# Block 0 of a graph attention's scores: masks by an identity matmul, the score bank copied by ScalarE, and a reordered opening

## Chip, cores and metric

One core of a Trainium2 chip runs the kernel. The metric is the time on the device in microseconds (us), as the median of several runs. Engines: TensorE (PE in the profile; PEld are its weight loads), VectorE (DVE), ScalarE (ACT), GpSimd (POOL) and SyncE (SP), whose queue issues all the DMAs.

## What is computed

One layer of graph attention over 4096 nodes of 256 features, followed by a feed-forward layer with eight experts. Cut to what matters here:

```python
h = layernorm(x)
lQ, lK, lV = masked_x @ Wlq, h @ Wlk, h @ Wlv + blv
s = where(adj, lQ @ lK.T / 16, -1e9)        # 4096 x 4096
g, e = (masked_x @ Wgq) @ (mean(h) @ Wgk).T / 16, masked_x @ Wes
m = maximum(max(s, 1), maximum(g, e))
le, ge, ee = exp(s - m), exp(g - m), exp(e - m)
den = sum(le, 1) + ge + ee
res = le/den @ lV + ge/den * gV + ee/den * eV
x1 = x + maximum(res, masked_x)
out = x1 + ffn(layernorm(x1))               # 8 experts, 256 -> 1024 -> 256
```

## The kernel before

The 4096 queries are cut into eight blocks of 512 (`CH`); for each block the 4096 keys pass in 32 tiles of 128 (`KT`). Step `t` makes one score tile, 128 keys by 512 queries, in one of three PSUM banks `s_ps[t % 3]` (`score`, L1528). Every fp32 product is split into a high part, rounded to the type fp32r, and a low remainder: `split_product` (L47) issues three matmuls for each half of the 256 features (L52, L53, L54), six for a score. The mask of a tile, `bias`, is 0 where the adjacency has an edge and a large negative number elsewhere; GpSimd makes it from bytes (`bias_of`, L696). VectorE adds it to the bank and writes the sum into a slot of `scores` (`mask`, L868), then folds it into the running maximum `kept_ps` (`keep`, L884). From step 37 on, the exponentials of the tiles (ScalarE, L1285 and L1291) and their products with the values (`weigh`, L1552 and L1559) run beside the scores of later blocks. The last block is followed by the experts.

Block 0 is different, and it is the first stage of the kernel: while its 32 scores are made, the keys themselves are still being made, in eight groups `g` of 512 nodes (`NG`), with four score tiles to a group. For group `g` the work goes through all engines:

- SP loads the rows, `load_x(g)` (L571), into one of two buffers `xg`.
- VectorE takes their moments (`first_moments`, L1129 and L1132), GpSimd the reciprocal deviation (`reciprocal_deviation`, L762 and L764, `rstd`), VectorE the product with the mean (`shift`, L1137, `nmr`).
- ScalarE normalises in four activations (`normalise`, L1443, line L1450, `lnf`), and writes the high part of the values (`high_values`, L1457, `vst`); GpSimd writes their low part in two halves (`low_values`, L776). SP stores `vst` to DRAM.
- TensorE transposes the rows through the identity, eight times 128x128 (`turn_keys`, L1762, into `u_ps`); ScalarE copies the two banks as high keys (L1469, `lnT_hi`), VectorE subtracts for the low keys (`low_turned`, L1153).

Each engine has its own program, an order written out by hand, and engines meet at semaphores only. The loops over `g` are at L619 (SP), L797 (GpSimd), L1176 (VectorE), L1466 (ScalarE) and L1781 (TensorE). In round `g` of its loop an engine works on the scores `t = 4g-4` to `4g-1` of the keys of group `g-1`, and on the keys of group `g` or of later groups. GpSimd's round is the mask of `t+2`, low values, the mask of `t+3`, low values, the mask of `t+4`, the reciprocal deviation of group `g+2`, the mask of `t+5`:

```python
low_values(g, 0); bias_of(t + 3); low_values(g, 1)
bias_of(t + 4); reciprocal_deviation(g + 2); bias_of(t + 5)
```

ScalarE's round is the high keys of `g`, `normalise(g + 1)`, which needs the reciprocal of group `g+1`, and `high_values(g)`.

Ahead of the loops stands an opening. The two query weights are multiplied to one matrix (`fold`, L1752), VectorE subtracts a column (`qw`, L1171), ScalarE and VectorE split it (`qw_hi`, `qw_lo`, L1465 and L1175). The masked tokens of block 0, `mg_raw`, are split too (`mg_hi` by ScalarE, L1300; `mg_lo` half by VectorE, L1144, half by GpSimd, L770), and `queries(0, m)` makes the queries of block 0 from them in twelve matmuls, into `mb_ps` and `mt_ps`; ScalarE and VectorE split those (L1304 and L1148). Then TensorE folds the key weights (`gw_ps`), makes a small attention column (`attc_ps`, L1795), transposes group 1, and begins the scores. The masked tokens of block 1 are loaded into the same `mg_raw` in round 1 (`load_masked`, L247) and split there; their queries follow in round 3. In round 1 VectorE also centres the value weights (L1215, L1217).

At the stage's end, after score 29, TensorE makes the mean's matmuls (L1812) and after score 31 the row products (L1820); VectorE takes the folded row `wg_b` (L1225) and goes on to the first maximum and the first exponentials.

## Time and profile before

| | |
|---|---|
| median of 3 runs | 1091.46 us (1090.68 to 1092.83) |
| the profiled execution | 1091.44 us, span 1089.6 us, granted clock 0.991 of full |
| TensorE | 1043.4 us busy, 96% of the span |
| VectorE | 864.3 us, 79% |
| GpSimd | 704.2 us, 65% |
| ScalarE | 542.7 us, 50% |
| bytes moved | 180.39 MB, 166 GB/s on average |
| first stage | from 0 to about 108 us; the first exponential of block 0 begins at 107.74 us |

All times in the trace count from the start of the span. A row of a timeline gives the start, the time, the engine, the line, the operation, the tensors written and read, and how many instructions were merged in it; where the engine stood idle before, how long and for whom stands in brackets. Start to start of two neighbours is what an instruction costs an engine that is never idle; the time of a single row is longer where instructions overlap.

### The profile page before, as it was taken

How to read it: one execution, taken by the hardware profiler on the slowest of the kernel's cores; microseconds unless marked ns; L12 is line 12 of the kernel's file. 1: busy time of each engine (PE TensorE's matmuls, PEld its weight loads, DVE VectorE, ACT ScalarE, POOL GpSimd, SP SyncE). 2: the span in 40 equal slices, each digit the busy share in tenths (PEclk: the TensorE clock that was granted, in tenths of full speed). 3: DMA queues.
4: the chain of work that ended last, by engine and by line, in shares of the span. 5: the costliest groups of instructions: out<-in, count | busy, mean ns of one | idle time of the engine just before them, and what ended most of it. 6: DMA issues, size and time to landing. Idle time of an engine off the chain costs nothing.

```text
span 1089.6 us, 15802 instructions
## 1 busy us (share of the span) xinstructions
PE 1043.4 (96%) x4996; PEld 869.2 (80%) x4996; DVE 864.3 (79%) x1534; ACT 542.7 (50%) x973; POOL 704.2 (65%) x713
## 2 busy tenths in 40 slices
PE   6878999999999999999999999998899999999998
PEld 5656887887887888788788788886787888898886
DVE  4999977798799789789879978987976775677653
ACT  4640444444445345444544444547467556655664
POOL 3774776767678677777767867768475455554451
PEclk9999999999999999999999999999899999999999
DMA  6585343453354345335335425449846547654621
GB/s 221 179 294 181 107 150 108 155 176 118 107 177 152 118 168 167 109 126 189 126 112 174 165 97 169 146 130 335 293 167 213 203 150 248 215 182 150 209 78 59
DMA packets 104341, 180.39 MB, mean 166 GB/s; under 512 B 14265, under 2 KB 45882, under 8 KB 104002
## 3 DMA queue, kind: packets, MB, share of 16 engines
q1 hardware_dynamic: 104258, 179.38, 48.8%
q8 instruction: 40, 0.66, 0.3%
q14 instruction: 43, 0.35, 0.1%
HBM read 143.63 MB, written 27.33 MB: 157 GB/s over the span
## 4 chain that ended last, share of the span: by engine, by line
PE 83%; DVE 5%; POOL 5%; DMA 3%; issue 2%; ACT 1%; SPq 0%; DVEq 0%; POOLq 0%; ACTq 0%
PE u_ps L1552 19%; PE s_ps L52 11%; PE s_ps L54 11%; PE s_ps L53 11%; PE u_ps L1559 9%; PE u_ps L52 3%; PE u_ps L54 3%; PE u_ps L53 3%; PE mt_ps L52 2%; PE mt_ps L54 2%; PE mt_ps L53 2%; POOL p_lo L709 2%; POOL m_lo L770 1%; PE s_ps L1607 1%; PE mb_ps L52 1%
## 5 line engine op out<-in xcount | busy, mean ns | idle before, releaser
L709 POOL TENSOR_TENSOR p_lo<-p_all,p_hi 128x512 fp32r<-128x512 f32 x224 | 295.4, 1319 | 171.8 <-PE u_ps L1559 105.2
L1285 ACT ACTIVATE p_hi<-scores 128x512 fp32r<-128x512 f32 x224 | 141.6, 632 | 360.3 <-DVE scores L866 360.0
L882 DVE TENSOR_TENSOR scores<-s_ps,bias 128x512 f32<-128x512 f32 x256 | 175.7, 686 | 84.0 <-PE s_ps L54 82.5
L1552 PE MATMUL u_ps<-p_hi,v_in 128*128 128x512 f32 x896 | 241.0, 391 | 0.0
L52 PE MATMUL s_ps<-q_hi,lnT_hi 128*128 128x512 f32 x512 | 203.0, 397 | 12.9 <-DVE scores L882 12.8
L54 PE MATMUL s_ps<-q_hi,lnT_lo 128*128 128x512 f32 x512 | 200.6, 392 | 0.0
L53 PE MATMUL s_ps<-q_lo,lnT_hi 128*128 128x512 f32 x512 | 200.4, 391 | 0.0
L1552 PEld LDWEIGHTS u_ps<-p_hi,v_in 128*128 128x128 f32 x896 | 167.2, 188 | 34.0
L701 POOL TENSOR_SCALAR bias<-adj 128x512 f32<-128x512 uint8 x256 | 164.2, 642 | 19.3 <-DVE scores L882 19.2
L866 DVE TENSOR_TENSOR scores<-scores,mb_ps 128x512 f32<-128x512 f32 x256 | 171.7, 677 | 0.8 <-PE mb_ps L1577 0.8
L903 DVE TENSOR_TENSOR kept_ps<-kept_ps,scores 128x512 f32<-128x512 f32 x232 | 162.3, 699 | 8.0
L1559 PE MATMUL u_ps<-p_lo,v_in 128*128 128x512 f32 x448 | 138.1, 389 | 0.2 <-POOL p_lo L709 0.2
L1291 ACT ACTIVATE p_all<-scores 128x512 f32<-128x512 f32 x224 | 138.0, 616 | 0.0
L731 POOL TENSOR_TENSOR e_lo<-raw,e_hi 128x512 fp32r<-128x512 f32 x64 | 84.2, 1319 | 73.5 <-ACT e_hi L1324 73.5
L52 PEld LDWEIGHTS s_ps<-q_hi,lnT_hi 128*128 128x128 f32 x512 | 96.7, 189 | 37.7 <-DVE scores L882 18.0
L54 PEld LDWEIGHTS s_ps<-q_hi,lnT_lo 128*128 128x128 f32 x512 | 96.8, 189 | 20.6
L53 PEld LDWEIGHTS s_ps<-q_lo,lnT_hi 128*128 128x128 f32 x512 | 96.9, 189 | 19.5
L1559 PEld LDWEIGHTS u_ps<-p_lo,v_in 128*128 128x128 f32 x448 | 84.0, 188 | 18.2 <-POOL p_lo L709 0.6
L52 PE MATMUL u_ps<-h_hi,e_hi 128*128 128x512 f32 x128 | 50.5, 394 | 0.1
L53 PE MATMUL u_ps<-h_lo,e_hi 128*128 128x512 f32 x128 | 50.4, 393 | 0.0
L54 PE MATMUL u_ps<-h_hi,e_lo 128*128 128x512 f32 x128 | 50.3, 393 | 0.0
L965 DVE TENSOR_TENSOR h_lo<-mb_ps,h_hi 128x512 fp32r<-128x512 f32 x32 | 22.1, 690 | 29.6 <-ACT h_hi L1324 29.6
(212 smaller groups left out, 1777.0 us busy)
## 6 DMA issues: line engine op xcount, KB each, us to landing
v_in<-v_scratch SPq DMA_DIRECT2D x118, 512.0 KB, 3.7
adj<-in_adj SPq DMA_DIRECT2D x64, 256.0 KB, 3.9
raw<-in_wffn SPq DMA_DIRECT2D x32, 512.0 KB, 4.9
v_scratch<-vst SPq DMA_DIRECT2D x8, 1024.0 KB, 6.2
mx<-in_mx SPq DMA_DIRECT2D x18, 256.0 KB, 6.8
xg<-in_x SPq DMA_DIRECT2D x8, 512.0 KB, 4.4
uhi_scratch<-uT_high SPq DMA_DIRECT2D x8, 512.0 KB, 2.7
ulo_scratch<-uT_low SPq DMA_DIRECT2D x8, 512.0 KB, 3.6
```

The source lines that it names most:

```text
L52: nc.tensor.matmul(out, l_hi, r_hi, start=start and k == 0, stop=False)
L53: nc.tensor.matmul(out, l_hi, r_lo, start=False, stop=False)
L54: last = nc.tensor.matmul(out, l_lo, r_hi, start=False, stop=stop and k == n - 1)
L701: nc.gpsimd.tensor_scalar(bias[:, t % 2], adj8[:, t // 4 % 2, t % 4 * CH:(t % 4 + 1) * CH], -MASKED, MASKED, ALU.mult, ALU.add).then_inc(b ...
L709: nc.gpsimd.tensor_tensor(out=low_part(y), in0=whole_part(y), in1=high_part(y).bitcast(fp32), op=ALU.subtract).then_inc(plo_ready, 1)
L866: nc.vector.tensor_tensor(scores[:, y % SLOTS], scores[:, y % SLOTS], mb_ps[:, :], ALU.subtract).then_inc(centred, 1)
L882: nc.vector.tensor_tensor(scores[:, t % SLOTS], s_ps[t % 3][:, :], bias[:, t % 2], ALU.add).then_inc(masked, 1)
L903: nc.vector.tensor_tensor(top_keys[:, :] if k == LASTS else kept_ps[:, :], kept_ps[:, :], scores[:, t % SLOTS], ALU.max).then_inc(kept, 1)
L1285: nc.scalar.activation(high_part(y), scores[:, y % SLOTS], ACT.Exp, scale=SCALE).then_inc(phi_ready, 1)
L1291: nc.scalar.activation(whole_part(y), scores[:, y % SLOTS], ACT.Exp, scale=SCALE).then_inc(pall_ready, 1)
L1552: nc.tensor.matmul(u_ps[d][:, :], values[:, x % 2, at:at + P], high_part(x), start=k == 0 and part == 0, stop=False)
L1559: last = nc.tensor.matmul(u_ps[d][:, :], values[:, x % 2, d * P:(d + 1) * P], low_part(x), start=False, stop=k == LASTS)
```

## The change

The masks of block 0 are written as fp32r into `turned_bias`, which lies where `bias` lies. `score` adds the mask by a seventh matmul into the same bank, with an fp32r copy of the identity, `ident_high`, as the weights. VectorE's `mask` falls away for block 0, and ScalarE copies the bank into its slot instead (`keep_score`). The masked value becomes a power of two. `bias_of` waits for the score two tiles back in place of its mask. `normalise` is cut into two halves with a copy between them.

The opening is put in another order. ScalarE begins with the masked tokens of block 0 and the identity's copy; the query weights' split goes by halves and stands ahead of `first_moments(1)` on VectorE; both halves of `mg_lo` of block 0 go to GpSimd, which also makes the masks of tiles 0 and 1 and the reciprocal deviation of group 2 ahead of its loop. The key weights' fold, the attention column and the transposes of group 1 go behind scores 0 and 1 on TensorE, in other banks. SP loads group 2's rows ahead of four weight matrices, after the first normalising. Centring the value weights goes from VectorE to GpSimd (`centred_values`). `first_moments(2)`, `shift` and `low_turned` change their places on VectorE, and the last of the first three value loads waits for score 31, as `ident_high` lies where it lands.

```diff
...
 SCALE = 1.0 / 16.0
-MASKED = -1.0e9 / SCALE
+MASKED = -float(2 ** 34)
 EPS = 1e-5
...
 bias = rings("bias", [P, 2, CH])
+turned_bias = nc.alloc_sbuf_tensor_at("turned_bias", [P, 2, CH], fp32r, offset=q_at + 8 * SLOT + 4 * CH * 2)
 mxt = rings("mxt", [P, D])
...
 vst = before("vst", [P, 2, TG, 2 * D], fp32r)
+ident_high = before("ident_high", [P, P], fp32r)
...
 tr_ps, q_ps = u_ps, [mb_ps, mt_ps]
-qw_ps, gw_ps, attc_ps = s_ps
+qw_ps, gw_ps, attc_ps = s_ps[0], mb_ps, mt_ps
...
 phi_ready, pall_ready, plo_ready, pv_done = (sem(n) for n in ("phi_ready", "pall_ready", "plo_ready", "pv_done"))
-late_low_ready = sem("late_low_ready")
+late_low_ready, ident_high_ready = sem("late_low_ready"), sem("ident_high_ready")
 turned, local_ready, top_ready, spread_ready, spread_done = (
...
         sp.dma_start(wq_in[:, n], kblocks(w)).then_inc(wg_loaded, 16)
+    sp.wait_ge(ln_ready, 1)
+    load_x(2)
     for n, w in enumerate((wlv, wev, attn_wT, next_wT)):
...
     sp.dma_start(blv_row[:, :], blv[None, :]).then_inc(wlv_loaded, 16)
-if g + 2 < NG:
+if 0 < g < NG - 2:
     sp.wait_ge(ln_ready, g + 1)
...
 for i in range(VRING):
+    if i == VRING - 1:
+        sp.wait_ge(score_done, KT)
     load_values(sp, i)
...
     pool.wait_ge(adj_in[g % 2], 16 * (g // 2) + 16)
-wait(pool, masked, t - 1)
-nc.gpsimd.tensor_scalar(bias[:, t % 2], adj8[:, t // 4 % 2, t % 4 * CH:(t % 4 + 1) * CH], -MASKED, MASKED,
+wait(pool, score_done if t < KT else masked, t - 1)
+nc.gpsimd.tensor_scalar(turned_bias[:, t % 2] if t < KT else bias[:, t % 2], adj8[:, t // 4 % 2, t % 4 * CH:(t % 4 + 1) * CH], -MASKED, MASKED,
                         ALU.mult, ALU.add).then_inc(bias_ready, 1)
...
+def centred_values():
+    pool.wait_ge(w_loaded, 64)
+    pool.wait_ge(wlv_loaded, 32)
+    for k in range(KD):
+        nc.gpsimd.tensor_tensor(out=w_all[:, WLV, k], in0=w_all[:, WLV, k], in1=wlv0_b[:, :],
+                                op=ALU.subtract).then_inc(wlv_ready, 1)
+    pool.wait_ge(wlv_ready, 2)
+    nc.gpsimd.tensor_copy(w_all[0:1, WLV, 0, :], blv_row[:, :]).then_inc(wlv_ready, 1)
 def low_weight_matrix(n):
...
 reciprocal_deviation(0)
-low_queries_input(0, 0)
+for k in range(KD):
+    low_queries_input(0, k)
+bias_of(0)
+bias_of(1)
 reciprocal_deviation(1)
+reciprocal_deviation(2)
 for g in range(NG + 1):
...
     low_values(g, 1)
-bias_of(t + 4)
-if g + 2 < NG:
+if g > 0:
+    bias_of(t + 4)
+if 0 < g and g + 2 < NG:
     reciprocal_deviation(g + 2)
-if g < NG:
+if 0 < g < NG:
     bias_of(t + 5)
...
     low_queries_input(1, 0)
+    centred_values()
 if g == 3:
...
 dve.wait_ge(bias_ready, t + 1)
-if t == 16:
-    dve.wait_ge(wlo_ready, 4)
-if t == 20:
-    dve.wait_ge(w_stored, 32)
 if t == 32:
...
 shift(0)
-first_moments(1)
 dve.wait_ge(qw_done, 1)
...
                             ALU.subtract).then_inc(qw_ready, 1)
-low_queries_input(0)
-dve.wait_ge(qwhi_ready, 1)
-nc.vector.tensor_tensor(qw_lo[:, :, :], qw[:, :, :], qw_hi[:, :, :].bitcast(fp32), ALU.subtract).then_inc(qwlo_ready, 1)
+for m in range(KD):
+    dve.wait_ge(qwhi_ready, m + 1)
+    nc.vector.tensor_tensor(qw_lo[:, m], qw[:, m], qw_hi[:, m].bitcast(fp32), ALU.subtract).then_inc(qwlo_ready, 1)
+first_moments(1)
 for g in range(NG + 1):
     t = 4 * g - 4
-    if g + 1 < NG:
-        shift(g + 1)
     if g == NG:
...
 for i in range(4):
+    if i == 0 and 0 < g and g + 1 < NG:
+        shift(g + 1)
+    if i == 0 and 1 < g < NG:
+        low_turned(g, 0)
+        low_turned(g, 1)
     if g > 0:
-        mask(t + i)
         keep(t + i)
-    if i == 0 and g < NG:
+    if i == (1 if g == 1 else 0) and g < 2:
         for k in range(KD):
             low_turned(g, k)
+        if g == 0:
+            shift(1)
     if i == 1 and 0 < g and g + 2 < NG:
...
         low_queries(0, k)
+    first_moments(2)
+if g == 1:
     dve.wait_ge(attc_done, 1)
...
     nc.vector.tensor_tensor(attc_c[:, :], attc_ps[:, 0:KD], attnb_c[:, :], ALU.add).then_inc(attcol_ready, 1)
-    first_moments(2)
-if g == 1:
-    dve.wait_ge(w_loaded, 64)
-    dve.wait_ge(wlv_loaded, 32)
-    for k in range(KD):
-        nc.vector.tensor_tensor(w_all[:, WLV, k], w_all[:, WLV, k], wlv0_b[:, :], ALU.subtract).then_inc(wlv_ready, 1)
-    dve.wait_ge(wlv_ready, 2)
-    nc.vector.tensor_copy(w_all[0:1, WLV, 0, :], blv_row[:, :]).then_inc(wlv_ready, 1)
 if g in (6, 7):
...
-def normalise(g):
+def keep_score(t):
+    act.wait_ge(score_done, t + 1)
+    if t == 16:
+        act.wait_ge(wlo_ready, 4)
+    if t == 20:
+        act.wait_ge(w_stored, 32)
+    nc.scalar.activation(scores[:, t], s_ps[t % 3][:, :], ACT.Copy).then_inc(masked, 1)
+def normalise(g, tiles=range(TG)):
...
     wait(act, vlo_ready, 2 * g - 2)
-    for j in range(TG):
+    for j in tiles:
         last = nc.scalar.activation(lnf[g % 2][:, j, 1:D], xg[:, g % 2, j, 1:D], ACT.Identity, scale=rstd[:, g % 2, j:j + 1],
                                     bias=nmr[:, g % 2, j:j + 1])
-    last.then_inc(ln_ready, 1)
+    if TG - 1 in tiles:
+        last.then_inc(ln_ready, 1)
...
+high_queries_input(0)
+act.wait_ge(ident_ready, 2)
+nc.scalar.activation(ident_high[:, :], ident[:, :], ACT.Copy).then_inc(ident_high_ready, 1)
 normalise(0)
-high_queries_input(0)
-act.wait_ge(qw_ready, 2)
-nc.scalar.activation(qw_hi[:, :, :], qw[:, :, :], ACT.Copy).then_inc(qwhi_ready, 1)
+for m in range(KD):
+    act.wait_ge(qw_ready, m + 1)
+    nc.scalar.activation(qw_hi[:, m], qw[:, m], ACT.Copy).then_inc(qwhi_ready, 1)
 for g in range(NG):
+    t = 4 * g - 4
+    if g > 1:
+        keep_score(t - 1)
+    if g == 1:
+        keep_score(0)
+        keep_score(1)
     for k in range(KD):
...
                              accum_out=xsum[:, k, g:g + 1]).then_inc(thi_ready, 1)
-    if g + 1 < NG:
-        normalise(g + 1)
     if g == 0:
...
             high_queries(0, k)
+    if g + 1 < NG:
+        normalise(g + 1, range(2))
+    if g > 1:
+        keep_score(t)
+    if g + 1 < NG:
+        normalise(g + 1, range(2, TG))
+    if g > 1:
+        keep_score(t + 1)
+    if g == 1:
         act.wait_ge(gw_done, 1)
...
             high_queries(1, k)
+    if g > 0:
+        keep_score(t + 2)
+for t in range(KT - 5, KT):
+    keep_score(t)
 for t in range(KT, STEPS):
...
 wait(pe, masked, t - 2)
+if t < KT and t % 4 == 0:
+    pe.wait_ge(tlo_ready, t // 2 + 2)
 ks = slice(k * P, (k + 1) * P)
-split_product(nc, s_ps[t % 3][:, :], [(lnT_hi[:, d, ks], lnT_lo[:, d, ks]) for d in range(KD)],
-              [(q_hi[:, n % 2, d], q_lo[:, n % 2, d]) for d in range(KD)]).then_inc(score_done, 1)
+last = split_product(nc, s_ps[t % 3][:, :], [(lnT_hi[:, d, ks], lnT_lo[:, d, ks]) for d in range(KD)],
+                     [(q_hi[:, n % 2, d], q_lo[:, n % 2, d]) for d in range(KD)], stop=t >= KT)
+if t < KT:
+    pe.wait_ge(bias_ready, t + 1)
+    pe.wait_ge(ident_high_ready, 1)
+    last = nc.tensor.matmul(s_ps[t % 3][:, :], ident_high[:, :], turned_bias[:, t % 2], start=False, stop=True)
+last.then_inc(score_done, 1)
...
 t = 4 * g - 4
-if g < NG:
+if g < NG and g != 1:
     turn_keys(g)
 if g == 0:
-    pe.wait_ge(qwlo_ready, 1)
+    pe.wait_ge(qwlo_ready, 2)
     queries(0, 0)
     queries(0, 1)
-    pe.wait_ge(wg_loaded, 32)
-    fold(gw_ps, gw_done)
-    pe.wait_ge(rows_loaded, 16 * 3)
-    pe.wait_ge(w_loaded, 64)
-    for m in range(KD):
-        for k in range(KD):
-            last = nc.tensor.matmul(attc_ps[:, m:m + 1], w_all[:, WATT, k, m * P:(m + 1) * P], lnb[:, k:k + 1],
-                                    start=k == 0, stop=k == KD - 1)
-    last.then_inc(attc_done, 1)
-if g == 1:
-    pe.wait_ge(gw_ready, 1)
-    pe.wait_ge(attcol_ready, 1)
 if g > 0:
...
     score(t + 1)
+    if g == 1:
+        turn_keys(1)
+        pe.wait_ge(wg_loaded, 32)
+        fold(gw_ps, gw_done)
+        pe.wait_ge(rows_loaded, 16 * 3)
+        pe.wait_ge(w_loaded, 64)
+        for m in range(KD):
+            for k in range(KD):
+                last = nc.tensor.matmul(attc_ps[:, m:m + 1], w_all[:, WATT, k, m * P:(m + 1) * P], lnb[:, k:k + 1],
+                                        start=k == 0, stop=k == KD - 1)
+        last.then_inc(attc_done, 1)
     if g == 3:
+        pe.wait_ge(gw_ready, 1)
+        pe.wait_ge(attcol_ready, 1)
         queries(1, 0)
```

## Rows read from the trace of the kernel before

**Rows 1.** The page's first part: busy time, share of the span, instructions.
```profile
PE 1043.4 (96%) x4996; PEld 869.2 (80%) x4996; DVE 864.3 (79%) x1534; ACT 542.7 (50%) x973; POOL 704.2 (65%) x713
```

**Rows 2.** Windows: stretch, length, busy time (instructions) of PE, PEld, DVE, ACT, POOL.
```profile
50.00:55.00 5.00, 5.00 (x28) 4.22 (x27) 4.90 (x14) 2.82 (x7) 4.22 (x6) 1.00 0.33 89
```

**Rows 3.** The page's costliest groups: the mask; busy us, mean ns, idle before.
```profile
L882 DVE TENSOR_TENSOR scores<-s_ps,bias 128x512 f32<-128x512 f32 x256 | 175.7, 686 | 84.0 <-PE s_ps L54 82.5
```

**Rows 4.** The chain that ended last, 45 to 56 us: start, time, what.
```profile
45.89 1.04 POOL rstd L764
46.95 0.59 DVE nmr L1137
...
48.07 1.57 ACT lnf_even L1450 x3
49.65 0.96 ACT vst L1457
50.67 1.29 POOL vst L776
51.97 0.58 POOL bias L701
52.55 1.18 POOL vst L776
53.84 0.62 POOL bias L701
54.74 1.04 POOL rstd L764
```

**Rows 5.** GpSimd's timeline: the reciprocal deviations of groups 3 and 7.
```profile
34.98 1.04 POOL L764 TENSOR_TENSOR rstd<-veps,mhalf 128x4 f32<-128x4 f32 x1
...
74.85 1.04 POOL L764 TENSOR_TENSOR rstd<-veps,mhalf 128x4 f32<-128x4 f32 x1
```

**Rows 6.** TensorE's timeline: two neighbouring score matmuls, and eight transposes.
```profile
49.10 0.39 PE L52 MATMUL s_ps<-q_hi,lnT_hi 128*128 128x512 f32 x1
49.33 0.39 PE L53 MATMUL s_ps<-q_lo,lnT_hi 128*128 128x512 f32 x1
...
51.83 1.03 PE L1762 MATMUL u_ps<-ident,lnf_even 128*128 128x128 f32 x8
```

**Rows 7.** ScalarE's timeline: two neighbouring copies of a whole bank; the isolated one.
```profile
18.63 0.60 ACT L1304 ACTIVATE q_hi<-mt_ps 128x512 fp32r<-128x512 f32 x1 [0.97 <-PE mt_ps L54]
...
50.50 0.58 ACT L1304 ACTIVATE q_hi<-mb_ps 128x512 fp32r<-128x512 f32 x1
50.98 0.58 ACT L1304 ACTIVATE q_hi<-mt_ps 128x512 fp32r<-128x512 f32 x1
```

**Rows 8.** Opening: transposes, queries' first and last matmul, first score, second masked tokens.
```profile
10.68 1.58 PE L1762 MATMUL u_ps<-ident,lnf_even 128*128 128x128 f32 x8 [0.50 <-ACT lnf_even L1450]
...
14.04 0.50 PE L52 MATMUL mb_ps<-mg_hi,qw_hi 128*128 128x512 f32 x1 [1.78 <-DVE qw_lo L1175]
...
17.97 0.63 PE L54 MATMUL mt_ps<-mg_hi,qw_lo 128*128 128x512 f32 x1
...
21.85 0.48 PE L52 MATMUL s_ps<-q_hi,lnT_hi 128*128 128x512 f32 x1
...
31.19 1.06 ACT L1300 ACTIVATE mg_hi<-mg_raw 128x1024 fp32r<-128x1024 f32 x1 [1.05 <-DMA mg_raw<-in_mxT]
```

**Rows 9.** Timelines of VectorE and ScalarE: the folded row, the first exponential.
```profile
99.47 0.42 DVE L1225 COPY wg_b<-mt_ps 128x256 f32<-128x256 f32 x1 [0.38 <-PE mt_ps L1820]
...
107.74 0.63 ACT L1285 ACTIVATE p_hi<-scores 128x512 fp32r<-128x512 f32 x1 [24.05 <-DVE scores L866]
```

**Rows 10.** TensorE after two idle gaps; below, a window (length, busy, granted clock).
```profile
39.34 0.80 PE L52 MATMUL s_ps<-q_hi,lnT_hi 128*128 128x512 f32 x1 [2.23 <-DVE scores L882]
...
63.79 0.50 PE L52 MATMUL s_ps<-q_hi,lnT_hi 128*128 128x512 f32 x1 [2.27 <-DVE scores L882]
...
16.00:17.00 1.00, 1.00 (x4) 0.50 0.93 324
```

## The prediction, made before the change was run

> **What bounds the kernel now.** I read the page first. TensorE is busy 1043.4 us, 96% of the span [rows 1], and the change touches only the stage at the start, the scores of block 0 (tiles 0 to 31), so the question is when that stage ends. Next come the windows: from 50 to 55 us VectorE is busy 4.90 of 5 us [rows 2], so it looks like the bound of the stage; one mask costs it 0.686 us [rows 3]. The chain of waits then shows a second bound of the same size [rows 4]. It is a ring through three engines that closes once per group of four tiles: GpSimd's reciprocal deviation (`rstd`), VectorE's shift (`nmr`), ScalarE's four normalising activations (`lnf`) and its high copy (`vst`), GpSimd's low values, mask, low values, mask, and the next reciprocal. Each row begins where the one above ends. The reciprocal ends at 46.93 and one turn later at 55.78: 8.85 us. In other groups VectorE comes late and stretches the turn: the reciprocals of groups 3 and 7 end at 36.02 and 75.89 [rows 5], 39.87 us for four turns, 9.97 each. So relieving VectorE pays only down to the ring's own length, and whatever enters the ring is paid in every turn.
>
> **What the change moves.** The 32 masks leave VectorE, 32 x 0.686 = 22 us; of its 8.85 us per turn about 6.1 are left, and it binds no more. In their place come an identity matmul and `keep_score`, a copy on ScalarE. The matmul is bounded by the spacing of matmuls of its shape, 0.23 us, and by twice that at half clock; I take 0.23, as the clock is full in most windows. A score is then 7 x 0.23 = 1.6 us, a turn of TensorE 4 x 1.6 + 1.0 for eight transposes = 7.4 us [rows 6], under the ring. The copy's bounds are 0.60 us, a whole row of such a bank, and zero, as nothing excludes that one hides in a wait; I take 0.48, the spacing of two neighbours [rows 7], since it stands between other activations. Two of the four copies sit in the ring, one between the halves of the normalising and one ahead of the high copy, as ScalarE goes through its work in order. The other two fall where it waits for the next reciprocal.
>
> **The new ring.** Reciprocal's end to ScalarE 0.65, normalising 2.0, two copies 0.96, high copy with hand-over 1.1, low values 1.3, mask 0.58, low values 1.3, mask 0.58, reciprocal 1.35 [rows 4, 7]: 9.8 us. Are the scores in time? With the reciprocal's end at 0, the group's first score ends at -0.4 and its copy can start at 1.65; the second ends at 1.2 and is wanted at 3.15. The third and fourth wait longer: GpSimd writes the fourth mask only after low values, at 6.6, and TensorE, done with that score's six products at 4.2, stands 2.4 us at the identity matmul, with the next group's transposes and scores queued behind it. That idle time hides the identity matmuls (0.9 us per turn); without it TensorE would need 7.4 us, still less than the ring. ScalarE's next item is the copy of that fourth score; behind it are queued the turned keys' high copies, done at 8.7, where normalising can't start before 10.4: 1.7 us to spare. A turn of 9.8 against 9.97: the steady part is nearly even.
>
> **The opening.** The masked tokens' copy comes first (1.06), then the identity's (0.25, between 0.48 and nothing), then normalising, so the first transposes move from 10.68 to 11.7. The query weights no longer wait behind group 1's moments, and both low halves of the tokens go to GpSimd, so the query products follow the transposes at once, at 13.2 in place of 14.04 [rows 8]. Twelve take 2.8 us at full clock, to 16.0; before, they ended at 18.6, the later ones in 0.63 us each. A copy 0.6, a low half 0.7, and what VectorE has queued ahead (moments of group 1, low turned keys, shift) end at 17.5; the first score starts at 17.7 in place of 21.85, as the fold of the key weights, the attention column and the second transposes now stand behind two scores. Those end at 20.9, transposes 21.9, two turned banks' copies 23.1 (0.6 each), normalising 25.1, the folded weights' copy 25.7, the high copy 26.65, and with the 5.3 us of GpSimd's part of the ring the reciprocal of group 3 ends at 32.0 in place of 36.0: 4.0 ahead.
>
> In the next turn ScalarE first meets the second block's masked tokens, whose copy began at 31.19 when their load landed [rows 8]. The load is issued some 1.4 us earlier, so 29.8 now; then that copy 1.06, two score copies, the turned keys and the ring, to 42.2, 4.7 ahead of 46.93. Three turns of 9.8 against 28.96 us (46.93 to 75.89) give back 0.45: group 7's reciprocal ends at 71.7, 4.2 ahead.
>
> **The rest of the stage.** From 75.89 to the folded row on VectorE at 99.47 are 23.6 us [rows 5, 9]. Now: the ring's part up to the fourth mask, and score 23's end, 6.85; transposes 1.0; two scores 3.2; copy, high copy, low values, mask and score 27's end 3.9; low values, mask, score 28's end 1.95; score 29 1.6; the mean's matmuls 0.8; two scores 3.2; row products and hand-over 1.9: 24.4. That gives back 0.8. From the folded row to the first exponential at 107.74 [rows 9] nothing changes. So the stage ends 3.4 us earlier.
>
> **The clock.** TensorE stood idle 2.23 us ahead of 39.34, and the next matmul took 0.80 us; it stood idle 2.27 us ahead of 63.79, and the next took 0.50. From 16 to 17 us the granted clock was 0.50, the lower level of 1.2 GHz [rows 10], after a gap of 1.78 us [rows 8]. So gaps of about 2 us end either way. A stretch at the lower level costs some 1.6 us of matmuls. The new opening has a gap of 1.7 us ahead of the first score: if the clock falls there, scores and transposes end 1.7 later, of which 1.3 lasts, the next turn being held by the load. Bounds 0 and 1.3; the rows fell both ways, so 0.6. In later turns such a stretch is hidden by the 1.9 us that the second score has to spare.
>
> The Trainium skill, "TensorE: Matmul & The Clock Gate", section "HAM oscillation — how this bites in real kernels", says that matmul bursts with a wait behind each can be put back to the lower clock in every round. By that rule the sum would be the slower rival's 1098 us, by the rows 1088.6; the trace agrees in one of the two gaps above 2 us.
>
> **Edits costed at nothing.** Group 2's rows and a wait of SP for the first normalising go ahead of the weights' loads, which land about 1 us later; the copy that wants them first comes at 19.6, a cover of some 0.5 us. `centred_values` on GpSimd instead of VectorE: two subtractions of 0.64 (half of low values' columns and time) to 1.3 us, hidden while ScalarE is at its copies ahead of group 2's high copy; without that cover up to 2.9 us enter one turn. The early masks run while GpSimd waits for group 1's moments. The last value load now waits for score 31, long before its first product. Masks as a matmul operand: 0.62 us as now, or at most 1.3 as low values write that type; I take 0.62, as the operation stays the same; at 1.3 two masks would add 1.4 per turn. The constant costs nothing.
>
> The profiled execution took 1091.44 us, 1.84 more than its span of 1089.6; the median is 1091.46, so no correction is due. 1091.44 - 3.4 + 0.6 = 1088.6 us.
>
> **Rivals.** *Nothing to be measured, 0.25.* ScalarE now carries score copies and keys behind the masked tokens' copy; if that load lands at 31.2 as before, the turn ends 1.4 later, and with the lower clock at the first score 0.7 of the gain is left: 1090.7. For it: the queue carries the same bytes in less time. Against it: the transfers ahead are issued earlier.
>
> *Slower, 0.13.* TensorE's clock falls in every turn. Its wait of 2.4 us for the fourth mask recurs in five turns. If the whole burst behind it (14 matmuls, eight transposes) ran at 1.2 GHz, it would be 3.8 us longer, and the group's second score would end at 5.0 instead of 1.2; past 3.15 it holds ScalarE, so 1.9 per turn, 9.5 in all: 1098. It decides once a burst loses over 1.9 us; the 1.6 of one stretch doesn't. This is the case of the skill's rule above.
>
> **How the numbers follow.** The forecast has 0.62. About 0.2%, 2.2 us, is what a measurement of this kernel can tell from no change. Some 0.07 of the forecast falls within that, where the clock's full 1.3 is paid (1089.3): faster 0.55, same 0.32, slower 0.13. Range: at the low end the sum without the clock, 1088.0, less 1.5, a third of what ten copies in the ring cost (4.8), in case some hide; at the high end just past no change, for masks a little longer than 0.62: 1086.5 to 1092.0. It leaves out the slower rival and little else.
>
> **What would show it.** Right: first score near 17.7; reciprocals ending near 32, 42, 52, 62 and 72; ScalarE without a wait inside the ring; TensorE waiting for a mask once per group; VectorE idle about a third of a turn; first exponential near 104.9. Wrong: turns under 9.3 us (copies hide) or over 10.5 (clock, or longer masks), or ScalarE held by the masked tokens past 31.

## The result, and the profile after

The change made the kernel slower. It took 1098.48 us (median of 6 runs, 1095.52 to 1101.11) where the kernel before took 1091.22 (6 runs), a ratio of 1.0071 with a 95% interval of 1.0055 to 1.0088. A second set gave 1.0054 (1.0033 to 1.0074). The forecast was 1088.6, in a range of 1086.5 to 1092.0. The execution whose profile follows took 1100.55 us, 2.1 above its median, with a span of 1098.5.

TensorE's busy time, of the changed kernel, for [rows 1]:

```profile
PE 1049.5 (96%) x5028; PEld 875.2 (80%) x5028; DVE 836.2 (76%) x1499; ACT 559.6 (51%) x1007; POOL 708.8 (65%) x717
```

The window from 50 to 55 us, for [rows 2] (length, then busy time and instructions of PE, PEld, DVE, ACT, POOL; granted clock, DMA share, GB/s):

```profile
50.00:55.00 5.00, 5.00 (x24) 4.08 (x23) 3.54 (x11) 3.70 (x7) 2.62 (x3) 1.00 0.17 66
```

VectorE is relieved as intended: 3.54 of 5 us in place of 4.90. GpSimd's timeline of the changed kernel shows the ring, for [rows 4, 5] (start, time, engine, line, operation, and in brackets the idle time ahead and what ended it):

```profile
35.17 1.03 POOL L770 TENSOR_TENSOR rstd<-veps,mhalf 128x4 f32<-128x4 f32 x1
36.28 0.68 POOL L707 TENSOR_SCALAR turned_bias<-adj 128x512 fp32r<-128x512 uint8 x1
37.05 1.29 POOL L776 TENSOR_TENSOR mg_lo<-mg_raw,mg_hi 128x512 fp32r<-128x512 f32 x1
...
46.88 1.04 POOL L770 TENSOR_TENSOR rstd<-veps,mhalf 128x4 f32<-128x4 f32 x1
48.00 1.32 POOL L707 TENSOR_SCALAR turned_bias<-adj 128x512 fp32r<-128x512 uint8 x2
52.22 1.30 POOL L782 TENSOR_TENSOR vst<-lnf_odd,vst 128x512 fp32r<-128x512 f32 x1 [2.90 <-ACT vst L1482]
53.60 0.62 POOL L707 TENSOR_SCALAR turned_bias<-adj 128x512 fp32r<-128x512 uint8 x1
54.30 1.29 POOL L782 TENSOR_TENSOR vst<-lnf_odd,vst 128x512 fp32r<-128x512 f32 x1
55.67 0.62 POOL L707 TENSOR_SCALAR turned_bias<-adj 128x512 fp32r<-128x512 uint8 x1
56.37 0.23 POOL L768 TENSOR_SCALAR veps<-mv 128x4 f32<-128x4 f32 x1
56.69 1.03 POOL L770 TENSOR_TENSOR rstd<-veps,mhalf 128x4 f32<-128x4 f32 x1
```

The reciprocal ends at 47.92 and again at 57.72: a turn of 9.80 us, where 9.8 was forecast and [rows 4] had 8.85. But group 3's ended at 36.20, where 32.0 was forecast and the kernel before had 36.02, and from group 3 to group 4 it took 11.72 us, not 10.2. ScalarE's timeline tells why, and ends with the first exponential, for [rows 8, 9]:

```profile
33.62 1.06 ACT L1316 ACTIVATE mg_hi<-mg_raw 128x1024 fp32r<-128x1024 f32 x1 [2.98 <-DMA mg_raw<-in_mxT]
34.59 1.06 ACT L1465 ACTIVATE scores<-s_ps 128x512 f32<-128x512 f32 x2
...
48.15 1.09 ACT L1474 ACTIVATE lnf_even<-xg,nmr,rstd 128x255 f32<-128x255 f32 x2 [1.39 <-DVE nmr L1155]
49.15 0.58 ACT L1465 ACTIVATE scores<-s_ps 128x512 f32<-128x512 f32 x1
49.63 1.08 ACT L1474 ACTIVATE lnf_even<-xg,nmr,rstd 128x255 f32<-128x255 f32 x2
50.61 0.58 ACT L1465 ACTIVATE scores<-s_ps 128x512 f32<-128x512 f32 x1
51.09 1.05 ACT L1482 ACTIVATE vst<-lnf_odd 128x1024 fp32r<-128x1024 f32 x1
...
111.12 0.63 ACT L1301 ACTIVATE p_hi<-scores 128x512 fp32r<-128x512 f32 x1 [9.46 <-DVE scores L888]
```

The second block's masked tokens land at 33.62, and the score copies wait behind their copy. From 48.15 to 52.04 ScalarE runs without a gap: that is the ring, and two score copies stand in it, 0.48 us apart from their neighbours. VectorE's timeline shows who waited for those copies, and what the last turn waited for:

```profile
35.20 0.70 DVE L921 TENSOR_TENSOR kept_ps<-kept_ps,scores 128x512 f32<-128x512 f32 x1 [6.38 <-ACT scores L1465]
...
37.07 1.28 DVE L1155 SCALAR_TENSOR_TENSOR nmr<-mv,rstd 128x4 f32<-128x4 f32 x1
...
47.95 0.16 DVE L1155 SCALAR_TENSOR_TENSOR nmr<-mv,rstd 128x4 f32<-128x4 f32 x1 [1.61 <-POOL rstd L770]
...
75.34 1.40 DVE L1147 BATCH_NORM_STATS2 st<-xg 128x6 f32<-128x256 f32 x4 [3.84 <-DMA xg<-in_x]
...
102.86 0.42 DVE L1241 COPY wg_b<-mt_ps 128x256 f32<-128x256 f32 x1 [0.48 <-PE mt_ps L1873]
```

The running maximum (`kept_ps`) idled 6.38 us for ScalarE, and the shift (`nmr`), queued behind it, came at 37.07, 0.87 after its reciprocal. At 75.34 the moments of group 7 waited 3.84 us for their tokens; the turn that holds them took 11.08 us. SyncE's queue has the issues of both loads:

```profile
27.05 0.38 SPq L591 DMA_DIRECT2D v_scratch<-vst  x1
27.47 1.60 SPq L249 DMA_DIRECT2D mg_raw<-in_mxT  x2
...
64.42 0.43 SPq L601 DMA_DIRECT2D whi_scratch<-w_high  x1
64.89 0.43 SPq L602 DMA_DIRECT2D wlo_scratch<-w_low  x1
65.37 1.11 SPq L573 DMA_DIRECT2D xg<-in_x  x1
```

The masked tokens' load goes out at 27.47 behind a value store that waits for GpSimd's low values; the load of group 7's tokens goes out at 65.37 behind both stores of the weights. TensorE's timeline gives the opening:

```profile
15.04 0.63 PE L53 MATMUL mb_ps<-mg_lo,qw_hi 128*128 128x512 f32 x1
15.47 0.63 PE L54 MATMUL mb_ps<-mg_hi,qw_lo 128*128 128x512 f32 x1
...
20.91 0.50 PE L52 MATMUL s_ps<-q_hi,lnT_hi 128*128 128x512 f32 x1 [1.41 <-DVE q_lo L1166]
```

The first score starts at 20.91, not 17.7. ScalarE's first activation is one cause: it stood 7.51 us waiting for the masked tokens of block 0, whose copy is now ahead of everything else there.

```profile
9.51 1.06 ACT L1316 ACTIVATE mg_hi<-mg_raw 128x1024 fp32r<-128x1024 f32 x1 [7.51 <-DMA mg_raw<-in_mxT]
```

The first exponential comes at 111.12, 3.38 later than in [rows 9]; the span is 8.9 longer.

The rest of the difference lies behind the stage, which the change was not to touch. GpSimd's timeline near 640 us, first of the kernel before, then of the changed one:

```profile
639.26 1.29 POOL L709 TENSOR_TENSOR p_lo<-p_all,p_hi 128x512 fp32r<-128x512 f32 x1 [2.20 <-PE u_ps L1559]
640.52 0.62 POOL L701 TENSOR_SCALAR bias<-adj 128x512 f32<-128x512 uint8 x1
```

```profile
639.84 1.29 POOL L715 TENSOR_TENSOR p_lo<-p_all,p_hi 128x512 fp32r<-128x512 f32 x1 [0.72 <-PE u_ps L1611]
641.22 0.62 POOL L707 TENSOR_SCALAR bias<-adj 128x512 f32<-128x512 uint8 x1
```

From the low part of the weights to the mask it takes 1.26 us before and 1.38 after, though both durations are the same, 1.29 and 0.62. About 0.11 us of nothing stands ahead of each mask, and as much behind it. A block's period (from one block's normalised sum, `uT`, to the next) is 91.78 us before (200.34 to 292.12) and 91.97 after (203.88 to 295.85); over the five periods up to 660 us that is 1.1 us. Behind 740 us this one profile loses another 4 us, which no other run shows in this size (e13 below).

### The profile page after: what moved, and what is told of

It is laid out like the page before. It is cut to its first block, busy times and chain, and to the rows that moved or that the text cites. A ratio compares the mean times of both kernels' runs of the same rounds, so it can differ in the third digit from the quotient of the medians.

```text
span 1098.5 us, 15893 instructions
## 1 busy us (share of the span) xinstructions
PE 1049.5 (96%) x5028; PEld 875.2 (80%) x5028; DVE 836.2 (76%) x1499; ACT 559.6 (51%) x1007; POOL 708.8 (65%) x717
## 4 chain that ended last, share of the span: by engine, by line
PE 65%; DVE 12%; POOL 7%; issue 7%; ACT 4%; DMA 4%; SPq 0%; DVEq 0%; POOLq 0%; ACTq 0%
PE u_ps L1604 13%; PE s_ps L52 8%; PE s_ps L54 8%; PE s_ps L53 8%; PE u_ps L1611 7%; DVE scores L888 3%; POOL p_lo L715 2%; PE u_ps L52 2%; PE u_ps L53 2%; PE u_ps L54 2%; ACT p_all L1307 2%; PE mt_ps L52 2%; DVE kt_out L989 2%; PE mt_ps L54 2%; PE mt_ps L53 2%
## 5 line engine op out<-in xcount | busy, mean ns | idle before, releaser
L900 DVE TENSOR_TENSOR scores<-s_ps,bias 128x512 f32<-128x512 f32 x224 | 153.8, 687 | 89.0 <-PE s_ps L54 87.5
L707 POOL TENSOR_SCALAR bias<-adj 128x512 f32<-128x512 uint8 x224 | 141.4, 631 | 27.3 <-DVE scores L900 5.8
L715 POOL TENSOR_TENSOR low_scores<-scores,p_late 128x512 fp32r<-128x512 f32 x23 | 30.9, 1357 | 23.3 <-ACT scores L1307 23.2
```

The lines of the kernel that those rows point to most:

```text
L707: nc.gpsimd.tensor_scalar(turned_bias[:, t % 2] if t < KT else bias[:, t % 2], adj8[:, t // 4 % 2, t % 4 * CH:(t % 4 + 1) * CH], -MASKED, ...
L715: nc.gpsimd.tensor_tensor(out=low_part(y), in0=whole_part(y), in1=high_part(y).bitcast(fp32), op=ALU.subtract).then_inc(plo_ready, 1)
L900: nc.vector.tensor_tensor(scores[:, t % SLOTS], s_ps[t % 3][:, :], bias[:, t % 2], ALU.add).then_inc(masked, 1)
```

## The experiments

Eight of the kernels answer three questions in all eight combinations (the cube, below): do the two ring copies stand in the ring, is the constant -2^34 or the old -1.6e10, are two loads late (as in the change) or early. "Tokens" is the start of the first masked tokens' copy, where ScalarE waits for their load, and "First exp." the start of the first exponential, in the one profile of each; the ratio is to the kernel before on the same chip, with its 95% interval. The medians of different rows come from different chips, so rows are compared by their ratios.

| run | masks on | copies in ring | constant | loads | median us (runs) | ratio | tokens | first exp. |
|---|---|---|---|---|---|---|---|---|
| before | VectorE | - | old | late | 1091.22 (6) | 1 | - | 107.74 |
| changed | TensorE | yes | -2^34 | late | 1098.48 (6) | 1.0071 (1.0055 to 1.0088) | 9.51 | 111.12 |
| e13, the same | TensorE | yes | -2^34 | late | 1096.79 (6) | 1.0054 (1.0033 to 1.0074) | 9.55 | 112.29 |
| e2 | TensorE | yes | old | late | 1094.57 (8) | 1.0031 (1.0017 to 1.0044) | 9.34 | 108.83 |
| e10 | TensorE | yes | -2^34 | early | 1092.65 (12) | 1.0026 (1.0008 to 1.0043) | 8.95 | 108.89 |
| e14 | TensorE | yes | old | early | 1090.47 (12) | 0.9996 (0.9984 to 1.0008) | 7.66 | 105.75 |
| e3 | TensorE | no | -2^34 | late | 1090.62 (11) | 0.9996 (0.9986 to 1.0007) | 8.55 | 105.50 |
| e15 | TensorE | no | -2^34 | early | 1088.67 (12) | 0.9993 (0.9978 to 1.0008) | 7.91 | 102.40 |
| e5 | TensorE | no | old | late | 1089.83 (12) | 0.9988 (0.9975 to 1.0000) | 8.84 | 107.92 |
| e9 | TensorE | no | old | early | 1085.05 (6) | 0.9950 (0.9932 to 0.9968) | 7.61 | 101.86 |
| e4 | VectorE | - | old | late | 1088.39 (12) | 0.9974 (0.9962 to 0.9986) | 7.80 | 104.11 |
| e6 | VectorE | - | old | early | 1087.30 (12) | 0.9965 (0.9952 to 0.9978) | 8.71 | 103.43 |
| e1 (kernel before) | VectorE | - | -2^34 | late | 1092.87 (11) | 1.0010 (0.9996 to 1.0023) | - | 109.06 |

The load of the first masked tokens is issued at 2.27 or 2.28 us in every profile that has a time there, and yet its tokens land between 7.61 and 9.55. No edit touches it. So first exponentials of single profiles can differ by up to 1.9 us for that reason alone.

**e1: the constant alone**, in the kernel before.

```
-MASKED = -1.0e9 / SCALE
+MASKED = -float(2 ** 34)
```

> The kernel before with one edit: the masked value is -2^34 instead of -1.6e10. In the changed kernel's trace every mask that GpSimd makes has a gap of some 0.11 us ahead of it and behind it, in the main loop too, where only the constant differs, and a block takes 91.97 us instead of 91.78. Theory A, the constant makes GpSimd's mask slower: the gaps and the 91.97 us appear here, the ring's turns grow by 0.4 us, and the time rises by some 2 to 3 us, to 1093 to 1094.5. Theory B, the mask's new output type or GpSimd's new order does it: no gaps, 91.78 us per block, 1091.

Measured: 1092.87 us, 1.0010. The gaps are there: low part to mask 1.39 us (637.57 to 638.96), period 91.96 in the mean of five. So the value of the constant makes the gaps; the edit changes two numbers of the mask's instruction and nothing else. Theory A's growth of the ring did not come: the turn from group 4 to 5 is 8.86 us, as with the old constant (8.85, [rows 4]); the last section says why. In total time e1 is not told apart from no change.

**e2: the changed kernel with the old constant**, the same line the other way.

> The changed kernel with the old masked value, -1.6e10 (rounded by the matmul, still far below any score). Theory A (constant): the gaps vanish, a block takes 91.78 us again, the ring's turn falls from 9.8 to 9.4 us, the time falls by 1.3 (blocks) plus 1.5 to 2 (stage), to some 1095. Theory B (type or order): gaps and times as in the changed kernel, 1098.5.

Measured: 1094.57 us, 1.0031, no gaps, period 91.78. The constant accounts for a part; 0.31 of the 0.71% is left. The turn did not fall to 9.4 us as theory A had it: from group 3 on the turns are 11.42, 10.23, 9.98 and 9.80.

**e3: the two ring copies behind the high copy** (constant of the change).

```
-                    if g + 1 < NG:
-                        normalise(g + 1, range(2))
-                    if g > 1:
-                        keep_score(t)
...
+                    if g + 1 < NG:
+                        normalise(g + 1)
...
                     high_values(g)
+                    if g > 1:
+                        keep_score(t)
+                        keep_score(t + 1)
```

> The changed kernel with one edit on ScalarE: both score copies that stand inside the ring (one between the halves of the normalising, one ahead of the high copy) go behind the high copy. Ring theory: a turn falls by 0.96 us from 9.8 to some 8.85; over five turns up to 4.8 less, of which the turn that waits for the last rows' load gives back one or two: 1094.5 to 1096. Rival, TensorE or the clock sets the turns: turns of 9.8 as before, 1098.5.

Measured: 1090.62 us, 0.9996: the loss is gone, and more of it than the 1094.5 to 1096 us expected. The turn from group 4 to 5 is 8.85 us (44.64 to 53.49), the ring of [rows 4] again. The three others, 10.80, 9.60 and 11.52, are not; and of the 5.6 us between this profile's first exponential and the changed kernel's, 2.4 lie ahead of group 3's reciprocal (33.84 against 36.20), where the edit changes nothing.

**e4: the opening alone**: the change's order of the opening, with masks and score tiles on VectorE as before, no identity matmul, no copies, the old constant.

```
-                        last = nc.tensor.matmul(s_ps[t % 3][:, :], ident_high[:, :], turned_bias[:, t % 2], start=False, stop=True)
...
+                            mask(t + i)
                             keep(t + i)
...
-                        keep_score(t)
```

> The changed kernel's opening, its loads' order and its GpSimd order, with the masks on VectorE as in the kernel before (no identity matmul, no score copies, old constant). If the opening as such gains nothing, because the masked tokens' load and the half clock hold it: the reciprocal of group 3 ends near 36 us and the time is 1090 to 1092; then the whole loss of the changed kernel comes from the masks' move and the constant. If the opening itself costs: over 1094. If it gains what the prediction said: 1088.

Measured: 1088.39 us, 0.9974. The opening by itself gains 2.8 us; the masks' way to TensorE, as the change has it, then costs 0.57% (e2 less e4), 6.2 us.

**e5: e3 with the old constant.**

> The changed kernel with both of its faults taken out: the two score copies of a turn stand behind ScalarE's high copy, outside the ring, and the constant is -1.6e10 again; masks still go through the identity matmul and the scores still come from ScalarE. Theory A (the two faults are all that the change loses): the constant was worth 1.8 us on the kernel before and 3.9 on the changed one, so some 2 to 3.9 us come off the 1090.6 us of the run with the copies behind: 1087 to 1088.6, at or below the 1088.4 of the opening alone; GpSimd's mask to the next mask's start 0.59 instead of 0.70 us; turns of about 8.85 us from group 4 on and a period of 91.78 us per block. Theory B (masks on TensorE are worse than on VectorE even outside the ring, because TensorE waits in order for GpSimd's mask and the bursts run at the lower clock): 1090 us or more, turns of 9.5 us or more, above the opening alone by over 1 us.

Measured: 1089.83 us, 0.9988, between the two theories. Without both faults the version still stands 0.14% above the opening alone, which the two intervals do not tell apart. Its turns point to loads: the masked tokens' copy begins at 32.98, and the last turn takes 11.95 us.

**e6: the opening alone, with two moves in SyncE's queue**: the second masked tokens' load ahead of the value store, the weights' stores behind the load of group 7's tokens.

```
                         load_x(g + 2)
+                    if g == 1:
+                        sp.wait_ge(q_done, 2)
+                        load_masked(sp, 1)
+                    if g == 5:
+                        sp.wait_ge(wlo_ready, 4)
+                        sp.dma_start(whi_dram, ...)
+                        sp.dma_start(wlo_dram, ...)
                     if g > 0:
                         sp.wait_ge(vlo_ready, 2 * g)
```

> The opening alone (masks on VectorE, old constant), with two moves in SP's queue: the second masked tokens' load is issued ahead of the value store instead of behind it, so some 4 us earlier (19.7 instead of 24.1 us), and the two stores of the weights go behind the load of group 7's tokens instead of ahead. Theory A (the loads hold the turns 2 to 3 and 6 to 7): the masked tokens' copy starts near 27.3 instead of 30.4 us, group 4's reciprocal ends 1 to 2 us earlier than 42.96, group 7's moments start 1 to 2 us earlier than 67.47; 1085 to 1087.5 us against 1088.4. Theory B (both loads are hidden, as the reciprocal of group 3 ended at 32.40 and hangs on GpSimd and VectorE, not on the masked tokens): the copy starts earlier and nothing behind it moves by over 0.5 us: 1088 to 1089.

Measured: 1087.30 us, 0.9965. The last turn is 8.85 us (62.41 to 71.26) in place of 10.09, and the four turns up to group 7 take 37.05 us in place of 39.56, but the time is only 0.09% better than e4's, less than the two intervals tell apart.

**e7, e8, e11, e12: which constants make the gaps**, in the kernel before, one run each: `MASKED` = -2^33, -1.7e10, -2^35, -2.0e10.

> The kernel before with the constant -2^33 in place of -1.6e10. It is a power of two like the change's -2^34, but smaller than the old constant. Theory A (a power of two as the immediate slows GpSimd's mask): the gap of 0.11 us on both sides of each mask is there, mask to next mask's start 0.72 us in the main loop, period 91.97 us per block, some 1093 us. Theory B (it is the size, or the exponent of 34): no gaps, 0.59 to 0.62 us, period 91.78, some 1091 us.

> The kernel before with the constant -1.7e10 in place of -1.6e10: no power of two, and close to the change's -2^34 = -1.718e10. Theory A (a power of two as the immediate slows GpSimd's mask): no gaps, period 91.78 us per block, some 1091 us. Theory B (the size decides, somewhere between 1.6e10 and 1.718e10, or any other constant than the old one does it): gaps of 0.11 us on both sides of each mask, period 91.97, some 1093 us. If neither this nor -2^33 shows gaps, the exponent of 34 or the value itself is left.

> The kernel before with the constant -2^35. Of -1.6e10, -1.7e10 and -2^33 none had the gaps around GpSimd's masks, -2^34 had. Theory A (from 2^34 on in size they appear): gaps of 0.11 us on both sides of each mask, period 91.97 us per block, some 1093 us. Theory B (only -2^34 has them): none, period 91.78.

> The kernel before with the constant -2.0e10, over 2^34 in size and no power of two. Theory A (from 2^34 on in size the gaps appear): gaps of 0.11 us on both sides of each mask, period 91.97 us per block, some 1093 us. Theory B (only a power of two from 2^34 on, or only -2^34): none, period 91.78, some 1091 us.

GpSimd's timeline, of e8 (-1.7e10) and of e12 (-2.0e10):

```profile
641.74 1.29 POOL L709 TENSOR_TENSOR p_lo<-p_all,p_hi 128x512 fp32r<-128x512 f32 x1 [0.84 <-PE u_ps L1559]
643.00 0.62 POOL L701 TENSOR_SCALAR bias<-adj 128x512 f32<-128x512 uint8 x1
```

```profile
642.01 1.29 POOL L709 TENSOR_TENSOR p_lo<-p_all,p_hi 128x512 fp32r<-128x512 f32 x1 [0.72 <-PE u_ps L1559]
643.39 0.62 POOL L701 TENSOR_SCALAR bias<-adj 128x512 f32<-128x512 uint8 x1
```

-2^33 and -1.7e10 leave 1.26 us from start to start, like -1.6e10; -2.0e10 and -2^35 leave 1.38 and 1.39, like -2^34. Being a power of two is not what counts: the gaps appear from some size between 1.70e10 and 1.718e10 (2^34) on. The periods go with them: 91.80 and 91.78 us without, 91.96 and 91.99 with. Each run's single time (1092.22, 1089.51, 1089.34, 1092.85) says nothing; runs of one kernel differ by more.

**e9: e5 with the early loads**, and **e10: the changed kernel with the early loads**, both by e6's edit.

> The changed kernel with the copies behind the ring, the old constant, and the two moves in SP's queue (second masked tokens' load ahead of the value store, weight stores behind group 7's load). Theory A (in the run with the copies behind and the old constant the masked tokens' copy at 32.98 us still held ScalarE's score copies, and the load of group 7 made the turn 6 to 7 11.95 us): both go, the copy starts near 29, group 4's reciprocal ends near 43, the last turn takes under 10.2; 1085.5 to 1087.5 us, level with the 1087.3 of the opening with early loads. Theory B (masks on TensorE cost by themselves, as the run without the loads' moves stood 1.4 us above the opening alone): 1088 to 1089.5 us, above the opening with early loads by 1 us or more.

> The changed kernel as it is, with only the two moves in SP's queue. Theory A (what the prediction's first rival named, the masked tokens' load that stands ahead of the score copies on ScalarE, is a part of the loss, 1.5 us, and the load of group 7, turn 11.08 instead of 9.8, another 1.3): masked tokens' copy near 29.5 instead of 33.6 us, group 4's reciprocal 2 to 3 us earlier against the first score, last turn 9.8 to 10; 1094.5 to 1096.5 us. Theory B (the loads are not on the path, all of the loss is the copies in the ring and the constant): 1097.5 us or more.

Measured: e9 1085.05 us, 0.9950, theory A, and the fastest of all; e10 1092.65, 1.0026. ScalarE's timeline of e10 (its load went out at 21.03):

```profile
29.02 1.05 ACT L1316 ACTIVATE mg_hi<-mg_raw 128x1024 fp32r<-128x1024 f32 x1
29.97 0.58 ACT L1465 ACTIVATE scores<-s_ps 128x512 f32<-128x512 f32 x1
```

The masked tokens no longer hold it: no wait stands ahead of 29.02, and the turns up to group 7 are 10.20, 9.80, 9.81 and 9.76 us where the change had 11.72, 9.80, 9.79 and 11.08. Those turns are 2.8 us shorter, as theory A had it; by time the loads' order is worth 0.28 or 0.45%, by which of the change's two ratios one takes.

**e13: the changed kernel again; e14: only the copies in the ring; e15: only the constant.**

> The changed kernel, unchanged, a second time. Theory A (its loss is steady and made up of the parts found): 5 to 8 us above the kernel before, and in this profile the stretch from the first exponential to the end is 981 to 984 us, as in all other profiles with or without the constant, not the 987.4 of its first profile. Theory B (the change costs something late in the kernel too): again 986 us or more for that stretch.

> The changed kernel with the old constant and the two moves in SP's queue, so that of the three suspects only the score copies between ScalarE's ring steps are left (two of the four of a turn). Theory A (ten copies of 0.48 us are paid in full, as the prediction had it): 4.8 us above the version with the copies behind and the same loads (0.995 of the kernel before), so 0.999 to 1.000 of the kernel before; turns of 9.8 us. Theory B (with the loads early most of them hide): within 2 us of 0.995; turns of 9.3 us or less.

> The version with the copies behind the ring and the early loads, with the constant -2^34 put back, so that of the three suspects only the constant is left. Theory A (the gaps cost 0.19 us in each of seven block periods and the shift that slips in ahead of the mask gives back in the ring what the gaps take): 1 to 2 us above 0.995 of the kernel before, so 0.996 to 0.997; turns as long as without it, within 0.2 us. Theory B (the gaps cost 0.46 us in each of the five turns too): 3 us or more above, 0.998 or more.

Measured: e13 1096.79 us, 1.0054. From its first exponential to its end are 984.7 us, between the theories: 2.7 less than in the change's first profile, 2.8 more than in the kernel before. Most of those 4 us came and went, so I don't count them as the change's. Its turns are 11.72, 10.23, 9.99 and 10.96 us: in the second, a copy in the ring waited for its score (0.17 us ahead of 48.45), which the first profile doesn't show.

e14 gave 0.9996, 0.46% above e9, 5.0 us: by its time theory A. Two reciprocals of e14, of groups 5 and 6, on GpSimd's timeline:

```profile
52.21 1.03 POOL L770 TENSOR_TENSOR rstd<-veps,mhalf 128x4 f32<-128x4 f32 x1
61.94 1.04 POOL L770 TENSOR_TENSOR rstd<-veps,mhalf 128x4 f32<-128x4 f32 x1
```

That is a turn of 9.74 us, in all four the same within 0.06. But e9, with the copies out of the ring, does not turn in 8.85 us: its turns are 9.28, 9.25, 10.12 and 9.42. From group 3's reciprocal to group 7's e14 takes 38.92 us and e9 38.07, 0.85 less, where eight copies paid in full make 3.84; another 2.27 lie between group 7's reciprocal and the first exponential (33.08 and 30.81). In e10 and e15, the same pair with the new constant, it is 1.54 and 3.66. So the copies cost what was forecast for them, within the intervals, but not by 0.96 us in every turn: without them something else sets the turn. VectorE's timeline of e9 shows it for group 6:

```profile
51.67 0.70 DVE L921 TENSOR_TENSOR kept_ps<-kept_ps,scores 128x512 f32<-128x512 f32 x1 [0.89 <-ACT scores L1465]
52.28 1.11 DVE L1155 SCALAR_TENSOR_TENSOR nmr<-mv,rstd 128x4 f32<-128x4 f32 x1
```

The reciprocal had ended at 51.51. The shift is queued behind the running maximum, which waits for the last score's copy on ScalarE, and begins 0.77 us late.

e15 gave 0.9993, by its time theory B, by its turns theory A: 33.86 to 71.89 is 38.03 us for four turns, and e9 took 38.07 (32.98 to 71.05). So the gaps do not lengthen the ring.

**The cube.** Each question has four pairs of runs that differ in nothing else (for the changed kernel the mean of its two ratios, 1.0063). Copies in the ring: 0.67, 0.33, 0.43 and 0.46%, in the mean 0.47%, 5.2 us. The constant: 0.32, 0.30, 0.08 and 0.43%, 0.28%, 3.1 us. The late loads: 0.37, 0.35, 0.03 and 0.38%, 0.28%, 3.1 us. With intervals of some 0.13% on each ratio, such a mean is uncertain by about 0.1%, 1.1 us. Together with e9's -0.50% the sum is 0.53%, against 0.71 and 0.54% measured: the three parts add up to the loss. The changed kernel is itself in a quarter of the pairs; without those pairs the sum is 0.43%, which the intervals still allow.

One thing the cube does not separate. In all four pairs for the loads the first masked tokens landed later in the profile with the late loads (by 0.6 to 1.7 us, 1.0 in the mean), and in all four pairs for the copies later with the copies in the ring (0.05 to 1.04, 0.6 in the mean), though neither edit comes before that landing; e4 and e6 differ the other way (7.80 and 8.71). With one or two profiles of a kernel it can't be told whether this is chance. If it isn't, up to 1.0 of the loads' 3.1 us and 0.6 of the copies' 5.2 belong to the landing.

## Why the prediction was wrong

**The ring's sum stood, and the price of what enters it in part by luck.** A turn of 9.8 was forecast; the two that no load stretched took 9.80 and 9.79 in the first profile, 10.23 and 9.99 in e13's, and 9.7 in e14. Ten copies at 0.48 us were priced at 4.8 us, and the runs gave 5.2 and, for e14 against e9, 5.0. But "whatever enters the ring is paid in every turn" did not hold: taken out again, the copies gave back 0.85 and 1.54 us over four turns, not 3.84, and 2.3 and 3.7 in the tail, where the forecast had two of the ten. VectorE was relieved. The tail from group 7's reciprocal to the folded row took 24.27 us, against 24.4, and 25.88 in e13. Of the edits costed at nothing, the masks kept their 0.62 us, and behind the centred values GpSimd still waited 1.58 us for ScalarE, so they were hidden.

**"The constant costs nothing" failed.** I took it for a number in an instruction and looked for no row, as the trace of before had none. It cost 3.1 us by the cube, uncertain by 1.1. The rows place 1.2 us of it: from the first exponential to the sixth `uT` the eight profiles with the gaps take 552.75 us in the mean and the nine without 551.56, and no profile of one kind reaches the other. From the first exponential to the end the means are 983.8 and 981.6, a difference of 2.2 us that is uncertain by some 0.8. In the ring the constant adds two gaps on each of two masks and takes them back by letting the shift in ahead of the next mask (below). Whether anything is left beyond that the runs don't tell.

**"The load is issued some 1.4 us earlier, so 29.8 now" failed.** The load went out at 27.47, 2.4 us later than before, and its tokens were wanted at 30.6, when ScalarE fell idle, and landed at 33.62. I followed the scores' chain in the opening and not the one that the load hangs on. SyncE issues it behind the value store, which waits for GpSimd's low values of group 0. These began at 24.00 (22.03 before) and took 3.03 us (2.55): ScalarE's high copy came 1.1 us later, behind the second query bank's copy and four normalising activations, and on GpSimd the change put group 2's reciprocal ahead of the low values, which waited for VectorE's moments until 22.67. The first rival, nothing to be measured, named this load, with the right victim (score copies queued on ScalarE) and 1.4 us for it. The forecast's own sign of being wrong, ScalarE held by these tokens past 31, came.

**The load of group 7's tokens had no term at all.** In the kernel before its turn took 10.06 us (65.83 to 75.89), of which VectorE waited 1.11 for that load; I spread this over four turns. The load hangs on SyncE's queue, behind an adjacency load and the weights' stores, which all moved later with GpSimd's masks, and so the turn took 11.08 us. Both loads together cost 0.28% by the cube. With the masks on VectorE the same moves gave 0.09% (e6 against e4), which may mean that they matter more for score copies on ScalarE; the intervals don't tell the two apart.

**The opening was 3.2 us late at the first score.** Transposes came at 12.87 (11.7 forecast), as the masked tokens' copy, now first, began at 9.51, when their load landed. The forecast put it ahead of the normalising, which had begun at 8.46, and gave that landing no term: in the kernel before the copy stood behind the normalising and no row showed it. Of the twelve query matmuls nine follow the one ahead by 0.42 or 0.43 us; from the first's start to the last's are 4.63 us (14.47 to 19.10), where eleven steps of 0.23 make 2.5. I had taken full clock, though [rows 8] showed 0.63 us for the last one in the kernel before. Where I did price the lower clock, at 0.6 us behind the gap ahead of the first score, it did not come: the gap was 1.41 us, and the matmuls behind it soon stood 0.23 apart. Group 3's reciprocal then came 15.3 us behind the first score, not 14.3: at 27.14 the normalising of group 2 had waited 0.95 us for the late low values of group 0, and it did so in e9 (0.96) and e14 (0.95) too. In e9 the first masked tokens were copied at 7.61, and its first score started at 17.70: so the forecast was that of the best case.

**What the forecast computed is e14**, with neither the constant nor late loads. There the first exponential came at 105.75, against 104.9, and group 7's reciprocal at 72.67, against 71.7. Yet its ratio is 0.9996 (0.9984 to 1.0008), -0.4 us against the -2.8 forecast. So of the 10 us between forecast and measurement the constant and the loads explain 3.1 each, 2.4 stand in e14 already, and the rest is within what the changed kernel's own two ratios differ by. Of the 2.4 the optimistic opening explains some 0.9, as far as e14's profile shows (first score at 18.46, 0.76 late; first exponential 0.85 late); the rest is about as large as e14's interval, 1.3 us, and no row places it.

**The slower rival had the time, 1098 us, and not the mechanism.** TensorE did wait for GpSimd's masks, but kept its clock. The changed kernel's groups of score matmuls between 20 and 111 us (count, busy us, mean ns):

```profile
L53 PE MATMUL s_ps<-q_lo,lnT_hi 128*128 128x512 f32 x74 | 28.9, 391 | 0.0
...
L1587 PE MATMUL s_ps<-turned_bias,ident_high 128*128 128x512 f32 x32 | 14.0, 438 | 13.2 <-POOL turned_bias L707 13.2
```

391 ns is the matmul of [rows 6], not the 0.63 us of the opening; the 13.2 us of waits, 2.1 us at most for one, stand at the identity matmuls, as forecast, and the matmuls behind them ran at full rate. The Trainium skill's section behind that rival ("TensorE: Matmul & The Clock Gate", "HAM oscillation — how this bites in real kernels") says that a matmul kernel whose bursts are followed by waits was put back to the lower clock in each of them. These turns don't show it; the waits of that example are longer, so they don't speak against it either, and the rival took it over too readily.

## What to carry to other kernels

Find the ring, price what enters it, and keep everything else of that engine behind the ring's step: the same copies behind ScalarE's high copy instead of ahead of it cost 5 us less (e9 against e14). Don't count on the price per turn, though: ask what sets the turn once the copies are gone. When work moves to another engine, follow every queue that waits for that engine, the DMA issues too, and write down for each load when it is wanted and on what its issue waits: two moves of loads were worth some 3 us. A constant is an edit like any other: compare the start-to-start distances of the instruction that carries it.

The best version here, e9, keeps the change's opening and the masks on TensorE, and takes its three faults out: 1085.05 us, 0.9950 (0.9932 to 0.9968). Against e6, which leaves the masks on VectorE (0.9965), its intervals overlap, so whether moving the masks is worth anything stays open.
